# Softmax sums and values in one pass of 64-row, 32-column tiles; the division between two block transposes

## Time and profile before

| | |
|---|---|
| three runs | 189.06, 189.95, 191.23 us; median 189.95 |
| the profiled execution | 191.24 us, of which the span of the records is 189.5 |
| PE busy | 177.6 us (94%) |
| PEld, DVE, ACT, POOL busy | 133.5, 133.4, 89.3, 86.2 us |
| mean granted clock of PE | 0.991 |
| chain of waits, by engine | PE 81%, DVE 8%, POOL 4%, ACT 2% |
| from 87.50 to 107.80 us (one middle step) | PE 20.30, DVE 14.52, ACT 9.86, POOL 8.27 us busy |

### The profile page before, as it was taken

How to read it: one execution, slowest core, us unless ns; L and a number is a source line. 1 busy time by engine, 2 the same in 40 slices (tenths; PEclk the granted TensorE clock), 3 DMA queues, 4 the chain that set the end, 5 groups by cost and what they waited for, 6 DMA issues and landing times.

```text
span 189.5 us, 3948 instructions
## 1 busy us (share of the span) xinstructions
PE 177.6 (94%) x1382; PEld 133.5 (70%) x1382; DVE 133.4 (70%) x375; ACT 89.3 (47%) x206; POOL 86.2 (45%) x112
## 2 busy tenths in 40 slices
PE   7999899988989999999999999999999995998884
PEld 2656483765878868886988788886878662587764
DVE  2678958797999586975697478838793776725661
ACT  3759779637263616454455626371525335303210
POOL 5589979758964504470427225340425023020300
PEclk9999999999999999999999999999999998799999
DMA  6999602010010301000020100010001000000111
GB/s 190 313 393 404 260 4 57 3 55 0 0 59 0 100 14 55 2 35 24 0 61 0 55 3 0 0 61 0 0 3 55 0 3 0 2 0 5 55 44 67
DMA packets 5331, 11.30 MB, mean 60 GB/s; under 512 B 688, under 2 KB 944, under 8 KB 5056
## 3 DMA queue, kind: packets, MB, share of 16 engines
q1 hardware_dynamic: 5024, 10.79, 16.4%
q10 hardware_dynamic: 288, 0.27, 0.4%
HBM read 8.95 MB, written 2.10 MB: 58 GB/s over the span
## 4 chain that ended last, share of the span: by engine, by line
PE 81%; DVE 8%; POOL 4%; issue 3%; ACT 2%; ACTq 0%; DVEq 0%; POOLq 0%
PE ps_w L996 12%; PE ps_w L997 11%; PE ps_w L1001 11%; PE ps_t L1009 7%; PE ps_s L1056 6%; PE ps_w L1153 4%; PE ps_s L1088 4%; PE ps_s L1094 4%; PE ps_s L1075 3%; PE ps_t L1014 3%; PE ps_w L1145 3%; PE ps_w L989 3%; DVE neg_top L731 3%; POOL b_lo L248 2%; PE ps_w L990 2%
## 5 line engine op out<-in xcount | busy, mean ns | idle before, releaser
L305 POOL TENSOR_TENSOR late<-late,gate 128x512 f32<-128x512 f32 x7 | 7.6, 1082 | 42.9 <-issue 27.8
L731 DVE TENSOR_REDUCE neg_top<-ps_s 128x8 f32<-128x512 f32 x32 | 20.0, 682 | 2.0 <-PE ps_s L1056 2.0
L483 ACT ACTIVATE eT<-ps_s 128x512 f32<-128x512 f32 x32 | 16.5, 605 | 4.3 <-PE ps_s L1081 4.2
L271 POOL TENSOR_TENSOR q_r<-q_a,q_b 128x512 f32<-128x512 f32 x7 | 9.1, 1295 | 17.3 <-DVE q_b L716 17.3
L996 PE MATMUL ps_w<-am_hi,x2T_hi 128*128 128x288 f32 x52 | 15.0, 310 | 1.6 <-ACT x2T_hi L504 1.6
L290 POOL TENSOR_TENSOR oT_lo<-o_n,oT_hi 128x512 fp32r<-128x512 f32 x8 | 10.2, 1276 | 12.5 <-ACT oT_hi L491 12.5
L996 PE MATMUL ps_w<-b_hi,zT_hi 128*128 128x512 f32 (+1 forms) x32 | 12.7, 401 | 1.9 <-ACT zT_hi L531 1.9
L997 PE MATMUL ps_w<-am_lo,x2T_hi 128*128 128x288 f32 x52 | 14.2, 296 | 0.0
L476 ACT ACTIVATE mT<-ps_t 128x256 fp32r<-128x256 f32 x8 | 3.1, 384 | 21.5 <-PE ps_t L1065 21.5
L996 PE MATMUL ps_w<-wo_hi,oT_hi 128*128 128x512 f32 x32 | 12.8, 401 | 0.0
L997 PE MATMUL ps_w<-wo_lo,oT_hi 128*128 128x512 f32 x32 | 12.6, 395 | 0.0
(11 more groups left out here) (192 smaller groups left out, 535.1 us busy)
## 6 DMA issues: line engine op xcount, KB each, us to landing
x_sb<-x SPq DMA_DIRECT2D x8, 256.0 KB, 7.4
cT_in<-cT SPq DMA_DIRECT2D x7, 256.0 KB, 3.2
out<-res SPq DMA_DIRECT2D x7, 256.0 KB, 2.0
wq_sb<-wq SPq DMA_DIRECT2D x4, 256.0 KB, 6.9
late<-wo SPq DMA_DIRECT2D x1, 1024.0 KB, 9.3
am_sb<-aT SPq DMA_DIRECT2D x1, 1024.0 KB, 8.3
b_sb<-bT SPq DMA_DIRECT2D x1, 1024.0 KB, 7.0
wkv_sb<-wkv SPq DMA_DIRECT2D x1, 512.0 KB, 4.6
```

The source lines that it names most:

```text
L271: pool.tensor_tensor(q_r[:].rearrange("p (r k d) -> p k r d", r=REP, k=KVH), q_a[:].rearrange("p (k r d) -> p k r d", r=REP, k=KVH), q_b[: ...
L483: act.activation(eT[:, c].rearrange("p b n -> p (b n)"), ps_s[:, c, :], ACT.Exp)\
L731: dve.tensor_reduce(neg_top[:, :, b, HALF_H * half:HALF_H * (half + 1)], ps_s[:, 2 * (1 - b) + half, :].rearrange("p (r h k) -> p r h k", ...
```

## The change

Sums and values come from one set of matmuls. `v_bd` is filled with ones and not zeros, so beside the 16 columns of a head's values stand 16 columns of ones. For each sequence, pair and head there is one matmul of 64 rows (the keys of that head) and 32 columns: 16 of its columns are the weighted values, the other 16 the sum. Head 0 of each pair writes bank 0, head 1 bank 1. `pair_ones`, its three POOL instructions and its semaphore go.

DVE transposes both banks in 32x32 blocks (`o_s`), takes two reciprocals, multiplies twice (`o_t`), and transposes back into `o_n`. The wait of `scores(t, 1)` for the banks is now for the first transpose (`o_step`) and not for `o_n`. The order of the steps on each engine is the same. `attend` gets a parameter `meanwhile` that no caller uses.

```diff
-        pair_ones = sb("pair_ones", [P, 2 * HD])
-        sum_t, inv_c, inv = sb("sum_t", [P, D]), sb("inv_c", [P, HD, 2]), sb("inv", [P, D])
-        o_n = sb("o_n", [P, D])
+        o_s, inv = sb("o_s", [P, 2, HD, 2, HD]), sb("inv", [P, 2, HD])
+        o_t, o_n = sb("o_t", [P, HD, 2, HD]), sb("o_n", [P, D])
-        ps_o, ps_sum = ps_s[:, 0, :], ps_s[:, 1, :]
+        ps_o = ps_s[:, 0:2, :]
...
-            pool.memset(v_bd[:], 0.0).then_inc(v_zero, 1)
+            pool.memset(v_bd[:], 1.0).then_inc(v_ones, 1)
...
-            pool.memset(pair_ones[:], 1.0).then_inc(ones_ok, 1)
...
-            def attend(t):
-                dve.wait_ge(sum_ps, t + 1)
-                dve.transpose(sum_t[:], ps_sum).then_inc(inv_step, 1)
-                dve.wait_ge(inv_step, 3 * t + 1)
-                dve.reciprocal(inv_c[:], sum_t[:].rearrange("p (u h d) -> p u h d", h=2, d=HD)[:, :, :, 0])\
-                   .then_inc(inv_step, 1)
-                dve.wait_ge(inv_step, 3 * t + 2)
-                dve.transpose(inv[:], inv_c[:].unsqueeze(3).broadcast_to([P, HD, 2, HD])).then_inc(inv_step, 1)
-                dve.wait_ge(inv_step, 3 * t + 3)
+            def attend(t, meanwhile=lambda: None):
+                n = 3 * t
                 dve.wait_ge(o_ps, t + 1)
+                dve.transpose(o_s[:].rearrange("p h u g d -> p (h u g d)"),
+                              ps_o.rearrange("p h n -> p (h n)")).then_inc(o_step, 1)
+                meanwhile()
+                dve.wait_ge(o_step, n + 1)
+                for h in range(2):
+                    mm = dve.reciprocal(inv[:, h, :], o_s[:, h, :, 1 - h, 0])
+                mm.then_inc(o_step, 1)
+                dve.wait_ge(o_step, n + 2)
+                for h in range(2):
+                    mm = dve.tensor_tensor(o_t[:, :, h, :], o_s[:, h, :, h, :],
+                                           inv[:, h, :].unsqueeze(2).broadcast_to([P, HD, HD]), ALU.mult)
+                mm.then_inc(o_step, 1)
+                dve.wait_ge(o_step, n + 3)
                 if t >= 1:
                     dve.wait_ge(oT_lo_ok, t)
-                dve.tensor_tensor(o_n[:], ps_o, inv[:], ALU.mult).then_inc(o_ok, 1)
+                dve.transpose(o_n[:], o_t[:].rearrange("p u g d -> p (u g d)")).then_inc(o_ok, 1)
...
                     if b == 0:
                         pe.wait_ge(exp_ok, 4 * t)
                     else:
-                        pe.wait_ge(o_ok, t)
+                        pe.wait_ge(o_step, 3 * t - 2)
...
             def values(t):
                 pe.wait_ge(exp_ok, 4 * t + 4)
-                for c in range(PAIRS):
-                    mm = pe.matmul(ps_sum[QUAD * c:QUAD * (c + 1), :], pair_ones[:],
-                                   eT[:, c].rearrange("p b n -> p (b n)"), start=True, stop=True)
-                mm.then_inc(sum_ps, 1)
                 pe.wait_ge(v_bd_ok, 4 * t + 4)
                 for b in range(2):
                     for c in range(PAIRS):
-                        mm = pe.matmul(ps_o[QUAD * c:QUAD * (c + 1), 2 * P * b:2 * P * (b + 1)],
-                                       v_bd[:, t % 2, b, c, :], eT[:, c, b, :], start=True, stop=True)
+                        for h in range(2):
+                            rows = slice(ROWS * h, ROWS * (h + 1))
+                            mm = pe.matmul(ps_o[QUAD * c:QUAD * (c + 1), h, 2 * P * b:2 * P * (b + 1)],
+                                           v_bd[rows, t % 2, b, c, :], eT[rows, c, b, :], start=True, stop=True)
                 mm.then_inc(o_ps, 1)
```

More of the change, by code:

```diff
@@ L165, in build @@
         warm_ok, ident_ok, mask_ok, pick_ok = sem("warm_ok"), sem("ident_ok"), sem("mask_ok"), sem("pick_ok")
-        ones_ok, sel_ok, const_ok, mask_step = sem("ones_ok"), sem("sel_ok"), sem("const_ok"), sem("mask_step")
-        v_zero = sem("v_zero")
+        sel_ok, const_ok, mask_step = sem("sel_ok"), sem("const_ok"), sem("mask_step")
+        v_ones = sem("v_ones")
         rope_step, cs_ok = sem("rope_step"), sem("cs_ok")
@@ L183, in build @@
         m_ps, mT_ok, sT_ps, exp_ok = sem("m_ps"), sem("mT_ok"), sem("sT_ps"), sem("exp_ok")
-        sum_ps, o_ps, inv_step, o_ok = sem("sum_ps"), sem("o_ps"), sem("inv_step"), sem("o_ok")
+        o_ps, o_step, o_ok = sem("o_ps"), sem("o_step"), sem("o_ok")
         oT_hi_ok, oT_lo_ok = sem("oT_hi_ok"), sem("oT_lo_ok")
@@ L334, in _ @@
                                channel_multiplier=1).then_inc(pick_ok, 1)
[L335 to L344, removed]
             def first():
@@ L448, in value_blocks @@
                 else:
-                    act.wait_ge(v_zero, 1)
+                    act.wait_ge(v_ones, 1)
                 for b in range(2):
@@ L1196, in second @@
                 raw_q(2, 0)
-                pe.wait_ge(ones_ok, 3)
                 values(0)
```

## The result

The changed kernel is slower: median 195.06 us (194.98 to 195.43, 4 runs) beside 190.59 us (189.06 to 191.29, 4 runs) for the kernel before on the same chip, ratio 1.0243 with a 95% interval of 1.0185 to 1.0301. The profiled executions took 195.08 and 191.24 us, spans 193.4 and 189.5, so 3.9 us are to be found in the traces. My 192.1 us with a range up to 194.2 was wrong. (Medians are of all executions; ratios leave out those in which a kernel fell in its slower state.)

A forecast was written before the change was run, and what follows sets the result against it. PE was taken to bound the kernel (busy 177.6 of 189.5 us), with DVE only about 0.8 us behind. Terms: 0.9 + 1.2 + 0.8 + 0 - 0.7 = +2.2 us, giving 192.1 on the median; range 185.5 to 194.2.

The forecast's parts named there:

- PE saves 0.86, the values take 1.0: PE, each tile: 32 passes in four rounds take 1.0 us where sums and values took 1.86.
- Rival C: PE's row halves do not overlap, so PE saves nothing; 191.3 us, chance 0.13.
- The division takes 3.26 undisturbed: DVE's new transposes, reciprocals and multiplies take 3.26 us a tile, 0.69 more than the 2.57 before.
- gated arrives inside the first multiply and gets in before the second; q_low ends at 94.15: Middle step, POOL against DVE: gated delays the second multiply to 92.8, and q_low ends at 94.15 where it was 93.24.
- Rivals A and B: A: DVE keeps the port over both multiplies, 188.2 us, chance 0.25; B: no clash that matters, 184.8 us, chance 0.12.
- The scores start 0.1 later than today, and turn_m another 0.1: PE, middle step: late q_low and late m_split each cost 0.1 us, +0.2 a step, +0.8 for tiles 2 to 5.
- DVE's own waits later in the step take up the rest: Middle step behind m_split: DVE's later waits absorb the remaining delay, so a step costs only +0.2 us.
- Tile 1, +1.2: First multiply meets b_lo's last piece, then gated; scores start 1.1 us later, and 0.1 comes at m_split.
- Tile 0, +0.9: First multiply meets am_lo's second piece on POOL; o_low and m_split's low part come later, shifting all by 0.9 us.
- Tile 6, gain 0: oT_hi would end at 152.7, while PE needs it at 152.83 less 0.86, so nothing is gained.
- Tile 7, -0.7: PE at half pace: sums and values fall from 3.6 to 2.0 us; output projection starts at about 165.8, not 166.51.
- a sum of its own: By the skill's weight-load rule PE would save 0.39 us a tile instead of 0.86, total about -0.5 us.

The follow-up runs named there:

- pe_padded: Changed kernel plus four more 128-row, 32-column matmuls a tile ahead of the values, which overwrite them; 194.78 us, 1.0288 of the kernel before, step 20.49.
- pad_before_rotate: Kernel before plus a spare 0.70 us DVE transpose just ahead of rotate_q in each middle step; 193.48 us, 1.0134 of the kernel before, step 20.80.
- os_psum_all: Changed kernel with the first transpose into PSUM for tiles 0 to 5 and o_low waiting for k_r; 187.26 us, ratio 0.9821; repeat 186.87, 0.9830.
- both_wait: Changed kernel; in middle steps POOL's gated waits for the division's multiplies and o_low for k_r; 191.33 us, 1.0038 of the kernel before, step 19.91.
- os_psum: Changed kernel with the first transpose into PSUM instead of SBUF for tiles 1 to 5; 190.03 us, 0.9986 of the kernel before, step 20.02.
- no_sums: Kernel before without the sum matmuls, divisors read from the values' bank, so not a softmax; 185.31 us, 0.9762 of the kernel before, step 19.47.
- os_psum_olow: Changed kernel with the first transpose into PSUM for tiles 1 to 5 and o_low waiting for k_r; 186.80 us, ratio 0.9810; repeat 187.95, 0.9873.

## Why the prediction was wrong

- *PE saves 0.86, the values take 1.0*: right. 1.09 us in the record, 1.02 to the next start, and 0.84 less than before. Rival C (row halves don't overlap) is excluded by this row.
- *The division takes 3.26 undisturbed*: right. In pe_padded it goes from 92.38 to 95.57 (o_n's transpose starts at 94.86 and takes 0.71), 3.19.
- *gated arrives inside the first multiply and gets in before the second; q_low ends at 94.15*: right. Counted from the values' start (87.47 in the earlier trace rows), gated is forecast 3.83 us and measured 3.86 us behind the values; the second multiply's end 5.33 and 5.24; q_low's end 6.68 and 6.56. Rivals A and B fall by the 1.32 us of the second multiply. The order that A supposed is to be seen in pe_padded, where gated comes 0.86 later.
- *The scores start 0.1 later than today, and turn_m another 0.1*: each was 0.0. These are the 0.2 that I put on a middle step.
- *"DVE's own waits later in the step take up the rest"*: **this step failed.** I had followed the delay up to m_split, found PE's next consumer, and stopped. Two instructions later stands q_b with 0.2 us of slack, and PE's `up_high` waits for it. From the end of m_split to q_b DVE has no wait at all, and between k_r and m_split one of 0.25 us: not enough for the 0.9 that k_r brings. pad_before_rotate shows what such a delay costs: +0.48 a step for 0.70 us. In the changed kernel a step grows by 0.56, where I had said that it would stay within 0.3; with tile 1 it is five such waits. Forecast for the middle steps was +0.8, measured +2.39.
- *Tile 1, +1.2*: measured +1.76. The scores are 1.15 late there (7.48 and 8.63 us behind the values; forecast 1.1), and most of the other 0.6 comes at `b_hi`, again at q_b. The same failed step. (My 53.60 for today's scores was the end of the record before them; they start at 53.53.)
- *Tile 0, +0.9*: +0.78, and os_psum_all takes back 0.70 of it by leaving SBUF: the mechanism (the multiply meets am_lo on POOL) is shown.
- *Tile 6, gain 0*: +0.10.
- *Tile 7, -0.7*: -1.56. The mechanism was right: the output projection now waits for oT_hi, 0.63 us. The size was off: I let the new values run at half pace, 2.0 us, and the profiled execution ran them at full clock. Busy time by stretch at the values of tile 7 in the kernel before (its sums, 1.94 us, are in the earlier trace rows) and in the changed one; PEclk, third from the right, is 0.53 and 1.00, the chip's 1.2 and 2.4 GHz levels:

```profile
159.65:163.20 3.55, 3.55 (x25) 1.04 (x25) 1.48 (x3) 0.54 (x1) 0.47 (x1) 0.53 0.00 0
```

```profile
165.08:166.20 1.12, 1.12 (x33) 0.59 (x34) 0.00 (x0) 0.55 (x1) 0.48 (x1) 1.00 0.00 0
```

Other profiles with this division part the two. Where they had the dip (both_wait, os_psum, os_psum_all), the values took 1.96 us and the output projection started 6.02 to 6.07 us behind their start; I had forecast 6.15, and the kernel before has 6.86. In the changed kernel's profile, without the dip, it is 5.20. So about 0.8 of the 1.56 is the change, as forecast, and the rest is a difference between two executions.

With the measured terms in place of mine the sum closes: 0.4 + 0.8 + 1.8 + 2.4 + 0.1 - 1.6 = 3.9 on the profiled execution's 191.24, and 195.08 was measured. On the median it is more, 4.5 to the 190.59 measured beside it: the kernel before was profiled in an execution that had the dip in the last tile. In the executions taken beside these experiments it ran 188.93 to 190.06 us at a mean clock of 1.00 and 190.63 to 191.98 at 0.991 (three more, at 0.982, 191.59 to 192.53), while the changed kernel's four runs lie within 0.45 us at either clock. Why its last values have no dip in the profile, after an idle time as long as before (2.16 and 2.18 us), no run here tells. Executions at full clock on both sides, 195.03 and 195.08 beside 188.93 to 190.06, put the cost of the change at 5 to 6 us. So the distance to my +2.2 is larger than the two profiled executions make it look.

My chances did not add up either: by their own terms "same" is 0.44 and "slower" 0.31, where I wrote 0.40 and 0.35.

The Trainium skill's rule (TensorE: Matmul & The Clock Gate, The mechanism), that weight loads overlap matmuls only in other row groups, was given a sum of its own in the prediction. By it the values would have taken some 0.47 us longer than 1.0. The trace disagrees: 1.02 us for 32 passes leave no room for four loads of 118 ns (106 in this trace). The same section also lets a load run ahead into a background weight buffer, which I had left out; whether that is what happens here no run tells.

## What to carry to other kernels

Follow a delay along its engine past the first consumer that is on time, to the next wait of the bounding engine, and write the slack down at each: a reuse of a bank is such a wait as much as a datum is. An elementwise step with both inputs in SBUF is priced by its neighbours on POOL, not by its length; in this kernel moving one scratch tile to PSUM and letting one POOL step wait turned +2.4% into -1.7%. And work taken from the bounding engine moves its consumers earlier, so ask what they will then run into.

## What the runs showed of the hardware beside this

- A DVE multiply of 256 f32 with one input in PSUM takes as long as with both in SBUF (two in 0.76 us in either), and a block transpose of 1024 elements from PSUM takes 1.24 us into SBUF and 1.26 into PSUM. So the way round the port costs DVE nothing. PE's next scores wait for the banks, which costs nothing in a middle step (5.84 us behind the values, as in no_sums) and 0.76 in tile 0 (3.81 and 3.05 in os_psum_all and os_psum_olow).
- PE's clock falls to half in some executions at two places of this kernel, near 41 to 49 us (granted clock 0.57 in the profiles of both_wait and os_psum, and some 2.6 us more between the first two tiles) and at the values of the last tile (0.53 in the kernel before, whose executions at a mean of 0.991 take some 2 us longer than those at 1.00). A comparison of totals to 1% must look at which of them the executions had; the length of a middle step is free of both.
